# A two-layer decoder on one core: second context part moved behind the first experts, idle products on TensorE, and four more edits

## The reference, cut to what matters

```python
x = ln(x + L0_attn(x))            # 16 heads of 16, half of them forward, half backward, ALiBi
x = ln(x + L0_xattn(x, ctx))      # queries from x, keys and values from the context; scores clipped
x = ln(x + L0_ffn(x))             # 8 experts, top 2, gelu(x w1) * (x v1), then w2
x = ln(x + L1_attn(x))            # 16 heads, every row sees every row
x = ln(x + L1_xattn(x, ctx))
x = ln(x + L1_ffn(x))             # rms norm, causal attention over a latent, rms norm, 8 experts top 2 (silu)
```

## Time and profile before

| | |
|---|---|
| three runs | 2084.49, 2091.39, 2094.41 us (median 2091.39) |
| profiled execution | 2086.37 us, span of the trace 2084.6 us |
| PE busy | 1872.3 us (90% of the span) |
| DVE busy | 1316.5 us (63%) |
| ACT busy | 1023.2 us (49%) |
| POOL busy | 518.6 us (25%) |
| granted TensorE clock | 0.94 of full speed in the mean |
| DMA | 157.94 MB, 76 GB/s in the mean |

### The profile page before, as it was taken

How to read it: one execution, slowest core, us unless ns; L and a number is a source line. 1 busy time by engine, 2 the same in 40 slices (tenths; PEclk the granted TensorE clock), 3 DMA queues, 4 the chain that set the end, 5 groups by cost and what they waited for, 6 DMA issues and landing times. The chain is left out here.

```text
span 2084.6 us, 35007 instructions
## 1 busy us (share of the span) xinstructions
PE 1872.3 (90%) x12192; PEld 1089.2 (52%) x12193; DVE 1316.5 (63%) x2305; ACT 1023.2 (49%) x1992; POOL 518.6 (25%) x869
## 2 busy tenths in 40 slices
PE   7899999797689999958999999987988999986992
PEld 4444445342679999934232222253453444476992
DVE  4688874698643333366888888556587888654114
ACT  3266666486212222243677777754643666632333
POOL 3211103333223332212000000222352101043551
PEclk9799999899789999988999999998998999977996
DMA  7554312520911111055221121055046234051224
GB/s 195 134 119 66 49 20 58 133 43 2 373 47 35 35 33 33 30 150 124 39 32 31 32 46 16 1 129 118 11 92 123 43 52 63 2 202 38 71 70 139
DMA packets 98874, 157.94 MB, mean 76 GB/s; under 512 B 31415, under 2 KB 78839, under 8 KB 93559
## 3 DMA queue, kind: packets, MB, share of 16 engines
q1 hardware_dynamic: 86898, 131.55, 27.4%
q0 software_dynamic: 7488, 20.46, 3.1%
q10 hardware_dynamic: 4352, 4.20, 0.6%
HBM read 110.44 MB, written 44.72 MB: 74 GB/s over the span
## 5 line engine op out<-in xcount | busy, mean ns | idle before, releaser
L1871 ACT ACTIVATE arena<-psum 128x512 f32<-128x512 f32 (+1 forms) x1120 | 578.3, 591 | 310.4 <-PE psum L1817 215.9
L1616 DVE TENSOR_REDUCE arena<-psum 128x1 f32<-128x1024 f32 (+7 forms) x384 | 431.0, 1159 | 92.1 <-PE psum L1574 56.7
L1817 PE MATMUL psum<-arena 99*128 99x512 bf16 (+7 forms) x1280 | 369.6, 352 | 8.7 <-DMA arena<-arena 6.3
L1574 PE MATMUL psum<-arena 96*128 96x512 bf16 (+7 forms) x1280 | 355.6, 361 | 15.1 <-SPq L2605 7.3
L2338 PEld LDWEIGHTS psum<-arena 128*128 128x128 f32 x2340 | 278.7, 195 | 7.4 <-ACT arena L2385 3.4
L2338 PE MATMUL psum<-arena 128*128 128x128 f32 x2340 | 280.0, 278 | 2.0 <-ACT arena L2385 1.4
L1835 PE MATMUL psum<-arena 128*32 128x512 f32 (+3 forms) x2560 | 280.7, 538 | 0.7 <-ACT arena L1871 0.7
L2431 DVE COPY arena<-arena 128x1536 f32 (+1 forms) x117 | 97.1, 830 | 287.1 <-PE psum L2338 284.3
L1602 DVE CUSTOM_DVE_ANT_0 arena<-psum,arena 128x1024 bf16<-128x1024 f32 (+3 forms) x224 | 217.4, 1020 | 49.1 <-PE psum L1574 48.9
L1817 PEld LDWEIGHTS psum<-arena 99*128 99x128 bf16 (+1 forms) x1280 | 120.4, 98 | 218.6 <-ACT arena L1871 122.4
L1574 PEld LDWEIGHTS psum<-arena 96*128 96x128 bf16 (+1 forms) x1280 | 109.6, 100 | 184.4 <-DVE arena L1616 47.4
(11 more groups left out here) (207 smaller groups left out, 2301.8 us busy)
## 6 DMA issues: line engine op xcount, KB each, us to landing
arena<-k_parts SPq DMA_DIRECT2D x144, 128.0 KB
q_halves<-arena SPq DMA_DIRECT2D x80, 192.0 KB, 2.9
arena<-q_halves SPq DMA_DIRECT2D x40, 384.0 KB, 4.8
arena<-in_L_ffn_up SPq DMA_DIRECT2D x8, 1408.0 KB, 17.1
arena<-q_halves SPq DMA_DIRECT2D x40, 256.0 KB, 5.3
k_parts<-arena SPq DMA_DIRECT2D x48, 192.0 KB, 3.1
arena<-in_L_ffn_down SPq DMA_DIRECT2D x9, 1024.0 KB, 13.4
arena<-y_rows SPq DMA_DIRECT2D x32, 256.0 KB, 4.0
```

The costliest lines, as they stand in the source:

```text
L1574: last = nc.tensor.matmul(dst[:, base + lo:base + hi], q[0:rows, qh, h, qb % 4 * P:qb % 4 * P + P], k[0:rows, h, key0 + lo:key0 + hi], sta ...
L1616: nc.vector.tensor_reduce(dst, src, AX.X, ALU.max).then_inc(t("taken"), 1)
L1817: last = nc.tensor.matmul(b[:, at0:at0 + width], kk[0:rows, h, kb * P:kb * P + P], q[0:rows, qh, h, c0:c1], start=True, stop=diag is None)
L1871: nc.scalar.activation(probs[k % at.ahead][:, heads[0]:heads[-1] + 1, c0:c1], bank[st_bank[no % 3]][:, 0:len(heads) * width].rearrange("p ...
```

## The change

Seven edits, as the diff shows:

1. The context part is divided by layer. t0 makes layer 0's keys and values, t3 makes layer 1's, whose weights and biases are loaded in t3 (`ctx1_loads`) into the tile `att`. at1 stores layer 1's values. The clear of the value tile goes from DVE to POOL (`pool_zero`), one layer at a time.
2. at0 is built without the 8: all 16 maxima of the first job, the transposition, the split and the DMA are part of t0.
3. In xa0 and xa1 the bias is added one tile of 128 tokens at a time, behind the split of each job (two behind the last), no longer all 16 behind the last split.
4. `keep_busy(n)` issues n products of the identity by itself into PSUM bank 2, of which nothing is read: 32 at the begin of t3, 20 at the begin of t7, and in both routings 36 behind the first two products and 22 behind the last.
5. In t7 the odd pairs are summed on PE: ACT makes diagonals of the gates, and PE adds x and the two experts' rows in PSUM, 6 products of 256 columns per pair; DVE's moments and ACT's norm read PSUM.
6. The planner's costs in the cross attentions change (clip 0.62 to 0.7, exponentials 0.59 to 0.7 and 0.61, maxima 0.75 to 0.8).
7. The costs and lags of the loads of the combining stages change; with edits 1, 2, 5 that gives t0, t3, t7 and at0 a new order.

```diff
-                clips.append(on_dve(exps[no], 0.62))
+                clips.append(on_dve(exps[no], 0.7))
...
-                free["ACT"] = max(free["ACT"], free["PE"] + 0.2, pvs[2 * j - 5] if j > 2 else 0.0) + 0.59
+                free["ACT"] = max(free["ACT"], free["PE"] + 0.2, pvs[2 * j - 5] if j > 2 else 0.0) + (0.7 if kind == "F" else 0.61)
...
-                taken.append(on_dve(free["PE"] + 0.2, 0.75))
+                taken.append(on_dve(free["PE"] + 0.2, 0.8))
...
+                    task("SP", "cload", 0, 5.0, 5.0, ("load", 5))
...
-                        task("SP", "load", p, 1.0, 5.0 if p < 4 else 3.5, ("add", p - 4))
-                    task("DVE", "add", p, 0.75 if source == "proj" else 1.9, 0.15, ("prj", p), ("load", p),
-                         (normed if not norm else "norm", p - 4), ("more", p - 4))
-                    task("DVE", "moments", p, 1.25, 0.15, ("add", p), ("square", p - 4))
+                        task("SP", "load", p, 1.0, 2.8 + 1.4 * p if p < 4 else 5.0, ("add", p - 4), ("sum", p - 4))
+                    if final and p % 2:
+                        task("ACT", "diag", p, 0.9, 0.15)
+                        task("PE", "sum", p, 2.6, 0.2, ("diag", p), ("load", p))
+                        task("DVE", "moments", p, 1.25, 0.15, ("sum", p))
+                    else:
+                        task("DVE", "add", p, 0.75 if source == "proj" else 1.9, 0.15, ("prj", p), ("load", p),
+                             (normed if not norm else "norm", p - 4), ("more", p - 4))
+                        task("DVE", "moments", p, 1.25, 0.15, ("add", p), ("square", p - 4))
...
-                    free = ("att", n_pairs - 1), ("add", n_pairs - 1), ("cmove", 7), ("cbias", 3)
+                    free = ("att", n_pairs - 1), ("add", n_pairs - 1), *context_ends(layer)
...
+            def on_pe(p):
+                return final and p % 2 == 1
+
+            def summed(eng, p):
+                if final:
+                    eng.wait_ge(t("prj_ps" if on_pe(p) else "r"), p // 2 + 1)
+                else:
+                    eng.wait_ge(t("r"), p + 1)
+
+            def row_of(u):
+                if on_pe(u // 2):
+                    return bank[u // 4][:, (u % 2) * D:(u % 2) * D + D]
+                return r_tok[:, u % TPB, :]
...
-                    sp.wait_ge(t("r"), p - 3)
+                    summed(sp, p - 4)
...
-                    nc.scalar.activation(x_tok[:, u, :], r_tok[:, u % TPB, :], ACT.Identity,
+                    nc.scalar.activation(x_tok[:, u, :], row_of(u), ACT.Identity,
                                          bias=rstd[:, 1, u % TPB:u % TPB + 1], scale=rstd[:, 0, u % TPB:u % TPB + 1])\
                         .then_inc(t("xs"), 1)
+
+            def act_diag(act, p):
+                for u in (2 * p, 2 * p + 1):
+                    for k in range(2):
+                        last = nc.scalar.activation(diag_of(u, k), ident, ACT.Copy, scale=gate_w[:, k, u:u + 1])
+                last.then_inc(t("diag"), 1)
...
+            def diag_of(u, k):
+                at0 = rest_base + 128 * (4 * (u // 4) + 2 * (u % 2) + k)
+                return arena[:, at0:at0 + P]
+
+            def pe_sum(pe, p):
+                pe.wait_ge(t("diag"), p // 2 + 1)
+                pe.wait_ge(t(f"rows{p % 4}"), 32 * (p // 4 + 1))
+                for u in (2 * p, 2 * p + 1):
+                    nc.tensor.matmul(row_of(u), ident, x_tok[:, u, :], start=True, stop=False)
+                    for k in range(2):
+                        last = nc.tensor.matmul(row_of(u), diag_of(u, k), gathered[:, k, u % TPB, :],
+                                                start=False, stop=(k == 1))
+                last.then_inc(t("prj_ps"), 1)
...
-                weights_ready(pe, wn)
+                if source == "comb":
+                    keep_busy(20 if final else 32)
+                if wn is not None:
+                    weights_ready(pe, wn)
...
-                task("DVE", "cclear", 0, 4.5, 0.15)
-                for n in range(len(self.kunits)):
-                    task("PE", "ckey", n, 1.1, 0.2, ("cload", 0), ("cbias", n - 2))
+            def tasks(self, task, layer):
+                task("POOL", "czero", 0, 2.2, 0.2)
+                task("DVE", "cclear", 0, 1.5, 0.15, ("czero", 0))
+                for n in (2 * layer, 2 * layer + 1):
+                    task("PE", "ckey", n, 1.3, 0.2, ("cload", 0), ("trx", 3), ("cbias", n - 2))
...
+                    if l == layer:
+                        task("PE", "cvalue", n, 1.3 if kb else 0.9, 0.2, ("ckey", 2 * l), ("cmove", n - 2))
+                        task("DVE", "cmove", n, 0.6, 0.15, ("cvalue", n), ("cclear", 0), ("cbias", 2 * l))
+
+            def load(self, sp, layer):
                 load_context_rows(sp)
-                load_weights(sp, self.wn)
+                if layer == 0:
+                    load_weights(sp, self.wn)
+                else:
+                    for dst, src in ctx1_loads:
+                        sp.dma_start(dst, src, allow_slow_non_contiguous=True).then_inc(sem(f"weights{self.wn}"), 16)
...
+                sp.wait_ge(t("v"), 4 * (l + 1))
+                sp.wait_ge(t("columns"), (1 + HG) * (l + 1))
+                sp.dma_start(vx_scr[l], self.vx[:, l].rearrange("p g b n w -> p (g b n w)"))\
+                    .then_inc(t("vstored"), 16)
...
+            def pool_zero(self, pool, l):
+                nc.gpsimd.memset(self.vx[:, l].rearrange("p g b n w -> p (g b n w)"), 0.0).then_inc(self.t("zero"), 1)
...
-                nc.vector.memset(vx.rearrange("p l g b n w -> p (l g b n w)"), 0.0).then_inc(t("zero"), 1)
-                dve.wait_ge(t("zero"), 1)
-                lanes = vx.rearrange("p l g b n w -> p (l g b) n w")
+                dve.wait_ge(t("zero"), l + 1)
+                lanes = vx[:, l].rearrange("p g b n w -> p (g b) n w")
...
-                if bias:
-                    add_bias(pool, *bias)
+                    if bias:
+                        add_bias(pool, *bias, (j - 1,) if j < NT - 1 else (j - 1, j))
...
+        def keep_busy(n):
+            for _ in range(n):
+                nc.tensor.matmul(bank[2][:, 0:P], ident, ident, start=True, stop=True)
...
+                keep_busy(36)
...
                 last.then_inc(t("found"), 1)
+                keep_busy(22)
...
-        at0 = SelfAttention("at0", ("fwd", "bwd"), True, q_halves, k_scr, 8)
+        at0 = SelfAttention("at0", ("fwd", "bwd"), True, q_halves, k_scr)
...
+                     ("v", w["wv"], w["bv"])], w, following=at0, layer=0)
...
+                     ("v", w["wv"], w["bv"])], w, following=at1, layer=1)
+        self_attention_stage(at1, (5, W["t4"]["brow"]), lambda sp: context.store_values(sp, 1),
+                             rows_free=lambda eng: context.values_stored(eng, 1))
...
+        def second_context(sp):
+            context.stored(sp, 1)
+            load_context(sp, 1)
```

More of the change, by code:

```diff
@@ L789, in make_plan @@
                 normed = "norm" if rms is None else "rms"
-                if context:
-                    task("SP", "cload", 0, 4.0, 3.0)
+                if layer is not None:
+                    task("SP", "cload", 0, 5.0, 5.0, ("load", 5))
                 for p in range(n_pairs if has_in else 0):
@@ L856, in make_plan @@
                         task("SP", "eload", 0, 1.6, 2.0, ("esplit", 0))
-                if context:
-                    context.tasks(task)
+                if layer is not None:
+                    context.tasks(task, layer)
                 return list_order(tasks)
@@ L934, in sp_prog @@
                     elif kind == "cload":
-                        context.load(sp)
+                        context.load(sp, layer)
                     elif kind == "cstore":
@@ L1002, in pool_prog @@
                         pool_add(pool, n)
+                    elif kind == "czero":
+                        context.pool_zero(pool, layer)
                     elif kind == "cthird":
@@ L1087, in act_prog @@
                         act_norm(act, n)
+                    elif kind == "diag":
+                        act_diag(act, n)
                     elif kind == "xts":
@@ L1183, in pe_prog @@
                         pe_prj(pe, n)
+                    elif kind == "sum":
+                        pe_sum(pe, n)
                     elif kind == "trx":
@@ L1299, in dve_prog @@
                 for kind, n in plan.get("DVE", []):
-                    rows = [r_tok[:, u % TPB, :] for u in (2 * n, 2 * n + 1)]
+                    rows = [row_of(u) for u in (2 * n, 2 * n + 1)]
                     if kind == "add":
@@ L1332, in token_stage @@
                 progs["undrained"] = "pool"
-            if units or source == "proj":
+            if units or source == "proj" or final:
                 progs["pe"] = pe_prog
```

90 lines of the change are left out of this document (45 added, 45 removed).

## The result

The changed kernel takes 2081.09 us in the median of 22 runs (2068.4 to 2086.6), the one before 2089.53 (2082.8 to 2096.9): ratio 0.9955, 95% interval 0.9943 to 0.9967. That is some 9 us less where 33 were forecast; 2081 lies above the range of 2040 to 2074.

A forecast was written before the change was run, and what follows sets the result against it. PE, 90% busy, was taken as the bound, with DVE's chain in the routings and DVE in t7. Terms -20 - 5 - 6 + 5 - 1 - 6 = -33 gave 2053.4 or 2058.4; forecast 2056 us, range 2040 to 2074.

The forecast's parts named there:

- t0 and at0 (-20): t0 and at0: moved context work and early maxima bring the first score product forward; 20 us gained, between 12 and 22.
- what is late next: at0: the second job's maxima go behind the first score and cost 3.5 us at full clock.
- xa0 (-5): xa0: spreading the bias additions gains a net 5 us, between 0 and 9.
- The step on edit 3: xa0: spread additions take away 9 us of stall, and clips that meet an addition give 4 us back.
- the new planner costs: I take 0, at most 4: xa0 and xa1: reordering leaves both engines' work the same; 0 us, at most 4 either way.
- each spread add costs what it takes: Rival for xa0: the spread bias additions gain 0 there, 2061 us in all; chance 0.09.
- Routings (-6): Routings and first expert tiles: idle products raise PE's clock; 6 us gained together, from below 2.
- t3 (+5 - 1): t3: moved context work adds 5 us, between 0 and 9.1; idle products ahead of the first units save 1.
- t7 (-6): t7: odd pairs summed on PE free DVE of 6.9 us; 6 us gained, from below 0 at half clock.
- the search gives back what the edits bring: Rival: new orders of at0, xa0, t0 and t3 are each a few us worse; same time, 2091 us; chance 0.03.
- Serial: Rival: context's 9.1 us stand wholly on t3's path, DVE adds 5, t0's last DMA lands late; 2074 us, chance 0.15.
- no clock: Rival: idle products don't lift the clock and are only work in routings, t3 and t7; 2079 us, chance 0.08.

The follow-up runs named there:

- edit 2 alone: The kernel before with all 16 maxima of at0's first job, transposition, split and DMA in t0, context work whole there: 2087.6 us, ratio 0.9997.
- edit 1 alone: The changed kernel with edits 2 to 6 taken back, leaving the context part divided by layer and edit 7's load costs in t3 and t7: 2084.5 us, 0.9977.

## Why the prediction was wrong

**t0 and at0 (-20).** The steps up to the first score product held: PE's work in t0 fell, at0's maxima began at 75.97 (forecast 74.4), and the first score product was 2 us off. The step that failed is "what is late next", which named the second job's maxima alone. Those cost 4 us (at0 took 244.0 us once nothing else was late, 240.1 before), near the forecast's 3.5. Late as well is group 1's load. It is issued as at0 begins, since its buffer holds t0's transposed input until t0 ends: at 80.0 before, at 74.3 with edit 1 alone, at 85.5 with edit 2 alone and at 78.8 with both. Without edit 2 the first score product stands 17 to 20 us behind that issue, with it 1 us ahead. So the 14.9 us by which edit 2 alone brings the first score product forward are lost again in at0, 7.3 of them in the wait for this load (0.9997), and what is left of 20 is edit 1's 9.4. With that load issued at 47 us the term is 18.2: what was forecast was there, behind a transfer that I had read only as something in the way of the first job's DMA.

**xa0 (-5).** The step on edit 3 was right: with the old costs -6 us in the stage (127.5 for 133.6), made of some 9 of stall and 2.5 to 3.5 paid back over the jobs, where 4 were forecast. The times leave its size open between 3 and 12 us. The step that failed is "the new planner costs: I take 0, at most 4": they cost 7 us in the lower profiles and up to 13, and by the time 12 (0.9955 against 0.9895). I had argued that as many draws are compared either way; but they are compared by the model's time, not the chip's. With the new order PE waits 7.1 us for the maxima's DMA, with the old one 2.1; why the model misses this was not tested. The rival "each spread add costs what it takes" looked right in the trace after (xa0 134.1, ten clips of 1.14 to 1.27 us and one of 1.97) and was wrong: with the clips free the time was the same. The Trainium skill's rule on the shared ports ("SBUF — State Buffer", section "SBUF: two separate sides") had the new order lose up to 9 us to it. In the trace an addition held one clip for some 0.5 us ten times, and taking even that away brought nothing.

**Routings (-6).** The 36 products were hidden (9.5 and 9.8 us) and raised the clock, as forecast. The step that failed is that the 22 run at full clock and fit into the wait for the fetched rows ("44 x 0.118 = 5.2 us"). The clock falls between the index products, so that the 22 take 6.9 and 7.5 us and not 5.2, and they delay DVE's next copies through the stage's end, for which I had allowed only 0.6 us. What the tiles gain (2.4 us in the first) is paid ahead of them. Measured: 0 within 4 us. The half-clock price of 0.19 us a record was misread too: 16 records reach into the 3 us of the earlier trace rows, but not all lie within it. From start to start a record takes 0.213 us at half and 0.112 at full clock in these traces. The rival without the clock counted +7 for the routings, where its own prices add up to +8.3.

**t3 (+5 - 1).** The context part costs 3 us by the profile of edit 1 alone. The idle products brought nothing: they reached full clock, and the first unit, 5.3 us behind their end, ran at half clock with them and without (5.68 and 6.25 us). The rule that the prediction cites from the Trainium skill ("TensorE: Matmul & The Clock Gate", "Part 4: PE-mode transpose") would give this; the transpositions and the waits between them are not told apart here.

**t7 (-6).** The stage became 4.8 us shorter in the profile (28.7 for 33.5), and 2.9 by the time of the variant without it, which is within the noise. DVE was freed of half its sums, as forecast. Whether this alone shortens the stage isn't shown, and the profiles speak against it: by one profile each it takes 32.0 us with the sums on PE and no idle products, and 31.8 with neither. In the range that the prediction gave, the case of sums at half clock ("from below 0") is near that one. Idle products without the sums on PE were not run.

The terms as measured: -9.4, +2 (xa0: 138.0 on average over eight profiles of the changed order, 135.8 over four of the old one), 0, +3, -5: -9.4 in all, against -9 measured. That they agree to under 1 us is luck, as one stage differs by 5 us between profiles of the same kernel. Of the rivals, "the search gives back what the edits bring" had the cause for xa0, but not for at0. "Serial" and "no clock" gave nearer times (2074 and 2079). Of "serial" the runs show nothing: t3 lost 3 us and not 14, and the first score product was early. Of "no clock" they show that the gain in the routings and in t3 is missing, but the clock did rise.

## What to carry to other kernels

When a stage's first work is pulled forward, list every load that its order needs in the next 20 us with its issue time, not only the first: the gain ends where the first transfer stands that can't be moved with it. When a planner's costs are changed, count it as a new order of unknown quality and time it alone; here costs nearer to the recorded durations gave a worse order. Idle products need two things that they lacked in the routings: nothing may wait for the stage's end behind them, and no wait may follow in which the clock falls again (here one of 3.45 us).

## What was not expected of the hardware

- The durations in the records overlap on DVE. In xa0 back-to-back clips last 0.68 us and begin 0.60 us apart, and reductions last 0.79 us and begin 0.71 apart. The new planner costs (0.7 and 0.8) are near the durations, the old ones (0.62 and 0.75) nearer to the spacing. That this is why the new order is worse was only argued.
- A pause of 1.7 us on PE between busy stretches was followed by 3.4 us at half clock in some places and by none in others. In the run of the changed kernel once more, three of five such pauses of xa0 were, and in its first profile the only one was not. The pauses recurred in every second job in some executions of the same order and not in others. Whether they make the 5 us between these profiles was not shown.
